# Issuing slot weights and padding from SyncE instead of GpSimd, with fewer VectorE steps in the routing of a two-layer mixture-of-experts block

## The chip, the cores and the metric

One core of a Trainium2 chip runs the whole kernel in one launch. The metric is the device time of that launch in microseconds (us), the median over runs.

## The reference

The input `x` has two sequences of 2048 tokens with 256 channels, all in float32. Three blocks follow one another; the first and the last use the same weights. Layer norms, softmax and gathers are left out here where they only repeat.

```
x = x + 0.5 * ffn(layernorm(x))
x = x + attention(layernorm(x))          # one head, 128 wide, causal
x = x + 0.5 * ffn(layernorm(x))

def ffn(x):                              # 4096 tokens, C = 256
    xln = ln(x, ln1)
    rwkv_state = xln @ Ws
    x = x + (sigmoid(xln @ Wr) * (xln @ Wv)) @ Wo
    h = ln(x, ln2)
    conf = sigmoid(h @ [conf_rwkv, conf_trans])            # 3 confidences
    bids = conf * capital_shares * sigmoid(h @ w_diff) + h @ W_aff
    win = argmax(bids)                                     # one of 3 experts
    wc = conf[win]; scale = wc / (wc + 1e-6)
    out0, out1 = relu(h @ K[e]) ** 2 @ V[e]                # hidden 1024
    out2 = (h @ W1 * sigmoid(rwkv_state @ W2)) @ W3
    return x + out[win] * scale
```

## The kernel before

**Precision.** Each float32 product is made of three passes over fp32r halves (`hi` and `lo`). A value is copied to its `hi` half by ScalarE, and VectorE or GpSimd subtracts to get the `lo` half. `passes` (L428) issues the three matmuls.

**Stages.** One pass of the feed-forward block has a front part, `ffn_a_*`, and a back part, `ffn_b_*`; attention stands between the two passes. The front part goes over eight groups of 512 tokens (`NG` = 8, four tiles of 128 each). It normalizes, makes the gated product, computes the bids and routes: VectorE's `gates(g)` finds the winner, counts it with a scan and casts flags and counts to bf16; TensorE's `prefix(g)` multiplies these with a triangle and with ones, so that each token gets a position; VectorE's `win(g)` computes the gate of the winner and `rank(g)` the row index. GpSimd's `scatter(g)` (L1602) then writes the token rows by four indirect DMAs to `routed`, a DRAM tensor with one region for each expert.

**Back part.** It goes over 18 slots (`NSLOT`), 16 of 256 rows of one expert and two of 128. The first eight (`EARLY_SLOTS`) are planned once five groups (`KNOWN`) are counted, so slots begin while groups 5, 6 and 7 are still routed: the code writes out by hand, on each engine, which step of which group stands between which steps of which slot. For each slot:

- SyncE loads the transposed operand's rows by `z_in(j)` (L1725, tile `slot_z`, semaphore `s_in`) and the residual rows by `row_in(j)` (L1742, tile `slot_row`, semaphore `r_in`). `z_in(0)` waits for the scatters of the first five groups.
- GpSimd loads half of the expert's first weight by `k_in(j)` (L1624, tiles `kx_hi` and `kx_lo`, 512 KB each, two buffers, semaphore `k_in`). It waits until TensorE is through with both halves of slot j-2.
- TensorE runs `sT(j)` (transposes, L770), `K(j, 0)` with weights held in SBUF, `K(j, 1)` with the loaded half, and later `V(j)`, the second product. Its order in the steady part is K(j), sT(j+1), V(j-1).
- ScalarE applies the relu, squares to `hr_hi`, and makes the transposed operand's `hi` half. VectorE computes `relu_squared` (L1463) and the third quarter's gate (L1473, L1475, L1477), the `lo` half of the transposed operand (`slo`, L1454) and the output row (`orow`, L1485 and L1487).
- GpSimd computes `hr_lo` in four quarters (`hrlo(j, n)`, L1674) and sends the output rows by indirect DMA (`send`, L1677). `V(j)` waits for the fourth quarter.

GpSimd's order in slot j from the third on is this; the drain stands there whether a load follows or not.

```
        hrlo(j, 0)
        hrlo(j, 1)
        hrlo(j, 2)
        pool.drain()
        if j + 2 < NSLOT:
            tail.k_in(j + 2)
        hrlo(j, 3)
        send(j - 1)
```

In slots 2 to 5 two tiles of a scatter follow the send, and in slot 5 the padding, `pads()` (L1611): three indirect DMAs of rows from SBUF that mark the end of each expert's region. The pad rows had been loaded to SBUF by SyncE (L1756), in the place of attention weights that come later. The slots from the ninth on need the late table (`late_tiles` to `late_numbers` on VectorE, semaphore `flag`), all scatters and the padding; SyncE waits for these before `z_in(8)`.

VectorE's `win(6)` follows `slo(3)`, and its `rank(6)` follows the gate of slot 2. TensorE's `T2(7)` (L507) waits for that rank. On VectorE a step wrapped in `link` (L1136) is followed by a wait for its own end.

Of the kernel before, what the change touches and what calls it, by code (L numbers as in the profile page):

```python
# [65 lines left out]
def build_kernel(nc, x, w256, w_st, w1, k_w, v_w, w_qkv, ln, shares, ident, tri, mask, tok, table, pad, out):  # L66
    with ExitStack() as ctx:
# [128 lines left out]
        b.oh = sb("winner_one_hot", [P, EXPERTS, GT + 1])  # L196
        b.cs = sb("winner_counts", [P, EXPERTS, GT + 1])
        b.won = sb("winner_conf", [P, EXPERTS, GT])
        b.rk = sb("winner_rank", [P, EXPERTS, GT])
        b.e16 = sb("winner_bf16", [P, EXPERTS * (2 * GT + 1)], BF16)  # L200
# [40 lines left out]
                 "posr", "rowz", "res", "link", "plink", "early", "padi", "pad_in", "flag",  # L241
# [243 lines left out]
def routing_tensor(pe, b, f, s):  # L485
# [645 lines left out]
def routing_vector(dve, b, f, n):  # L1131
# [28 lines left out]
    def gates(g):  # L1160
# [12 lines left out]
        link(dve.tensor_tensor(w(2), w(0), won(2), ALU.max))  # L1173
        link(dve.tensor_scalar(won(0), w(2), 0.5, None, ALU.is_lt))
# [4 lines left out]
        m = EXPERTS * GT  # L1179
        dve.tensor_copy(by_expert(b.e16[:, 0:m]), b.oh[:, :, 1:GT + 1])  # L1180
        dve.tensor_copy(by_expert(b.e16[:, m:2 * m]), b.cs[:, :, 0:GT])
        dve.tensor_copy(b.e16[:, 2 * m:2 * m + EXPERTS], b.cs[:, :, GT]).then_inc(f["e"], 1)

    def win(g):
# [4 lines left out]
        link(dve.tensor_tensor(w(3), b.won[:, 0], b.won[:, 1], ALU.add))  # L1189
        link(dve.tensor_tensor(w(3), w(3), b.won[:, 2], ALU.add))  # L1190
# [363 lines left out]
def ffn_a_gpsimd(pool, b, f, routed, s=None, a=None):  # L1554
# [56 lines left out]
    def pads():  # L1611
        pool.wait_ge(f["padi"], 1)
        pool.wait_ge(f["pad_in"], 16)
        for e in range(EXPERTS):
            pool.indirect_dma_start(routed, bass.IndirectOffsetOnAxis(b.padi[:, e:e + 1].bitcast(U32), 0), b.pad[:], None
                                    ).then_inc(f["padded"], 16)

# [46 lines left out]
def ffn_b_gpsimd(pool, b, f, dst, tail, s=None):  # L1664
# [35 lines left out]
    for j in range(2, NSLOT):  # L1700
# [12 lines left out]
        if j == 5:  # L1713
            tail.pads()
# [748 lines left out]
```

## Time and profile before

| what | value |
|---|---|
| median of 3 runs | 1028.52 us (1027.5 to 1028.8) |
| profiled execution | 1029.34 us |
| its span | 1027.6 us |
| mean granted TensorE clock | 0.95 |
| TensorE matmul busy | 88% of the span |
| VectorE busy | 71% |
| ScalarE busy | 57% |
| GpSimd busy | 54% |

Everything that is counted below comes from the one profiled execution. About 1.7 us of its time lie outside its span. The first feed-forward pass lies at 0 to 409 us, attention at 409 to 640, and the second pass from there to the end; in each pass the front part takes about the first 130 to 155 us.

### The profile page before, as it was taken

How to read it: one execution, taken by the hardware profiler on the slowest of the kernel's cores; microseconds unless marked ns; L12 is line 12 of the kernel's file. 1: busy time of each engine (PE TensorE's matmuls, PEld its weight loads, DVE VectorE, ACT ScalarE, POOL GpSimd, SP SyncE). 2: the span in 40 equal slices, each digit the busy share in tenths (PEclk: the TensorE clock that was granted, in tenths of full speed). 3: DMA queues.
4: the chain of work that ended last, by engine and by line, in shares of the span. 5: the costliest groups of instructions: out<-in, count | busy, mean ns of one | idle time of the engine just before them, and what ended most of it. 6: DMA issues, size and time to landing. Idle time of an engine off the chain costs nothing.

```text
span 1027.6 us, 20302 instructions
## 1 busy us (share of the span) xinstructions
PE 902.7 (88%) x6490; PEld 835.0 (81%) x6490; DVE 733.9 (71%) x1871; ACT 590.2 (57%) x1279; POOL 559.1 (54%) x656
## 2 busy tenths in 40 slices
PE   7998767979899999789998899888868988899997
PEld 6786657978899999678887688667658878899997
DVE  4679988669866664466676677679997769766663
ACT  3776736644566654355653655777756554555663
POOL 3447657866777775551122001256765775777774
PEclk8988988999999999899999999999998999999999
DMA  7215147454565542310111122303236463755542
GB/s 264 114 64 193 63 179 226 145 173 167 202 212 179 166 145 73 94 57 11 63 63 42 42 66 69 113 22 123 119 140 210 145 212 129 240 167 166 165 152 67
DMA packets 72975, 134.58 MB, mean 131 GB/s; under 512 B 7422, under 2 KB 54398, under 8 KB 72704
## 3 DMA queue, kind: packets, MB, share of 16 engines
q0 software_dynamic: 19232, 73.75, 21.1%
q1 hardware_dynamic: 53632, 59.42, 17.8%
q8 instruction: 62, 1.02, 0.4%
q14 instruction: 49, 0.40, 0.1%
HBM read 89.81 MB, written 44.64 MB: 131 GB/s over the span
## 4 chain that ended last, share of the span: by engine, by line
PE 26%; DVE 18%; ACT 5%; issue 4%; POOL 4%; DMA 2%; POOLq 0%; DVEq 0%; SPq 0%; another core or an unknown queue 0%; ACTq 0%
PE bank L431 16%; PE banks4to L431 4%; PE banks4to L2003 3%; DVE pT_lo L2293 2%; ACT p L2163 1%; PE bank L2015 1%; DVE chunk_max L2283 1%; POOL attn_x L2391 1%; DVE relu_squared L1463 1%; DVE state_gate L1475 1%; POOL routed_rows L1608 1%; DVE bn_parts L1362 1%; PE banks4to L770 1%; DMA routed_rows<-out_rows,row_index 1%; ACT pT_hi L2172 1%
## 5 line engine op out<-in xcount | busy, mean ns | idle before, releaser
L1674 POOL TENSOR_TENSOR hr_lo<-relu_squared,hr_hi 128x512 fp32r<-128x512 f32 (+1 forms) x144 | 179.6, 1260 | 65.1 <-DVE relu_squared L1463 53.0
L431 PE MATMUL bank<-v_hi,hr_hi 128*128 x544 | 156.3, 287 | 8.7 <-POOL hr_lo L1674 8.0
L431 PE MATMUL bank<-v_lo,hr_hi 128*128 x544 | 153.4, 282 | 2.8 <-issue 1.7
L431 PE MATMUL bank<-v_hi,hr_lo 128*128 x544 | 153.6, 282 | 0.8 <-issue 0.7
L1463 DVE TENSOR_TENSOR relu_squared<-relu 128x512 f32<-128x512 f32 (+1 forms) x108 | 102.3, 962 | 36.9 <-ACT relu L1023 20.4
L431 PEld LDWEIGHTS bank<-v_hi,hr_hi 128*128 128x128 f32 x544 | 103.5, 190 | 11.0 <-issue 10.9
L1049 ACT CAST hr_hi<-relu_squared 128x512 fp32r<-128x512 f32 (+1 forms) x36 | 21.4, 596 | 148.1 <-DVE relu_squared L1477 148.1
L1454 DVE TENSOR_TENSOR slot_zT_lo<-banks4to,slot_zT_hi 128x512 fp32r<-128x512 f32 (+1 forms) x68 | 42.0, 655 | 89.1 <-ACT slot_zT_hi L1003 79.1
L431 PEld LDWEIGHTS bank<-v_lo,hr_hi 128*128 128x128 f32 x544 | 103.2, 190 | 1.9 <-issue 1.9
L431 PEld LDWEIGHTS bank<-v_hi,hr_lo 128*128 128x128 f32 x544 | 103.5, 190 | 0.8 <-issue 0.6
L1608 POOL DMA_INDIRECT routed_rows<-out_rows,row_index x64 | 66.8, 1043 | 44.7 <-DVE row_index L1205 28.5
L1023 ACT ACTIVATE relu<-bank,slot_k_bias,slot_relu 128x256 f32<-128x256 f32 (+1 forms) x144 | 71.6, 548 | 28.9 <-PE bank L431 13.8
L1570 POOL TENSOR_SCALAR rsqrt_work<-mean_var 128x4 f32<-128x4 f32 x16 | 5.5, 343 | 148.6 <-DVE mean_var L1120 148.4
L431 PE MATMUL bank<-slot_zT_hi,kx_hi 128*128 128x256 f32 (+1 forms) x288 | 82.3, 286 | 0.0
L431 PE MATMUL bank<-slot_zT_hi,kx_lo 128*128 128x256 f32 (+1 forms) x288 | 81.8, 284 | 0.0
L431 PE MATMUL bank<-slot_zT_lo,kx_hi 128*128 128x256 f32 (+1 forms) x288 | 81.4, 283 | 0.0
L2163 ACT ACTIVATE p<-banks4to,minus_row_max 128x512 f32<-128x512 f32 (+2 forms) x80 | 49.8, 629 | 35.4 <-DVE minus_row_max L2286 28.7
L1036 ACT ACTIVATE hr_hi<-relu 128x512 fp32r<-128x512 f32 (+1 forms) x108 | 66.1, 612 | 5.6 <-POOL out_rows L1598 3.4
L2172 ACT CAST pT_hi<-bank 128x512 fp32r<-128x512 f32 (+1 forms) x72 | 39.2, 565 | 39.7 <-PE bank L2015 39.2
L431 PE MATMUL bank<-zT_hi,w_hi 128*128 128x512 f32 x96 | 44.5, 464 | 18.3 <-DVE r_gate L1342 13.1
L2293 DVE TENSOR_TENSOR pT_lo<-bank,pT_hi 128x512 fp32r<-128x512 f32 (+1 forms) x72 | 47.0, 658 | 18.9 <-ACT pT_hi L2172 18.3
L1475 DVE SCALAR_TENSOR_TENSOR state_gate<-relu,slot_relu,state_gate 128x512 f32<-128x512 f32 (+1 forms) x36 | 54.8, 1523 | 1.8 <-ACT relu L1025 0.5
(334 smaller groups left out, 3152.1 us busy)
## 6 DMA issues: line engine op xcount, KB each, us to landing
kx_hi<-first_product_halves POOLq DMA_DIRECT2D x36, 512.0 KB
kx_lo<-first_product_halves POOLq DMA_DIRECT2D x36, 512.0 KB
slot_z<-routed_rows SPq DMA_DIRECT2D x60, 256.0 KB
slot_row<-routed_rows SPq DMA_DIRECT2D x30, 258.0 KB
attn_x<-x_after_ffn SPq DMA_DIRECT2D x16, 256.0 KB, 2.9
attn_out<-x_after_ffn SPq DMA_DIRECT2D x16, 256.0 KB, 2.7
x_after_attention<-attn_out SPq DMA_DIRECT2D x16, 256.0 KB, 2.1
x_rows<-x_after_attention SPq DMA_DIRECT2D x8, 512.0 KB, 4.4
```

What stands on the lines that cost most here:

```text
L431: mm = pe.matmul(outv, w(pw), m(pm), start=(n_first and k == 0), stop=(n_last and k == 2))
L1023: last = act.activation(b.r[n % 2][:, h, 0:m], raw, ACT.Relu, bias=b.kb[:, j, at:at + 1], scale=b.fl[:, j:j + 1])
L1036: act.activation(b.hr[j % 2][0][:, 2 * q:2 * q + 2, 0:m], b.r[n % 2][:, :, 0:m], ACT.Square).then_inc(f["hrhi"], 1)
L1454: dve.tensor_tensor(b.sh[j % 2][1][:, part, :, 0:n], slot_bank(b, j, part).rearrange("p (c n) -> p c n", c=CC)[:, :, 0:n], b.sh[j % 2][0][ ...
L1463: dve.tensor_tensor(b.sq[n % 2][:, :, 0:width(j)], one, one, ALU.mult).then_inc(f["sq"], 1)
L1475: r.link(dve.scalar_tensor_tensor(gate, one, b.fl[:, j:j + 1], gate, ALU.mult, ALU.max))
L1608: pool.indirect_dma_start(routed, bass.IndirectOffsetOnAxis(b.posi[g % 2][:, t:t + 1].bitcast(U32), 0), b.rows[g % 2][:, t, :], None).then ...
L1674: pool.tensor_tensor(b.hr[j % 2][1][:, 2 * q:2 * q + 2, 0:m], b.sq[n % 2][:, :, 0:m], b.hr[j % 2][0][:, 2 * q:2 * q + 2, 0:m].bitcast(F32) ...
L2003: mm = pe.matmul(out[:, at:at + n], b.kq[pw][:, q, 0, t * P:(t + 1) * P], part, start=(k == 0 and i == 0 and not last), stop=(k == 2), ski ...
L2163: act.activation(b.p[s % 2][t][:, c * KEYS:c * KEYS + w], bank(("S", s, t, c))[:, 0:w], ACT.Exp, bias=b.nbias[:, s % 2, t:t + 1], accum_ou ...
L2172: act.copy(b.pT[m % 2][0][:, 0:w], b.bank(m % 2)[:, 0:w]).then_inc(a["pthi"], 1)
L2293: dve.tensor_tensor(b.pT[m % 2][1][:, 0:w], b.bank(m % 2)[:, 0:w], b.pT[m % 2][0][:, 0:w].bitcast(F32), ALU.subtract).then_inc(a["ptlo"], 1)
```

## The change

SyncE takes over `k_in` and `pads` from GpSimd. `k_in(j)` stands behind `z_in(j)` in SyncE's order. `pads` becomes three direct DMAs from DRAM to DRAM, at a row read into a register. The pad rows' copy in SBUF, its load and its semaphore go. In `gates`, the flag of expert 0 is formed in one step from the other two; flags and counts now lie in one tile, which is cast to bf16 by one copy in place of three. `prefix` reads that tile by other views. In `win`, one reduction takes the place of two additions.

```
-    pool.wait_ge(f["early"], 1)
...
-    k_in(0)
     rowz(NG - 2)
-    k_in(1)
     rs2(NG - 2)
...
     hrlo(0, 1)
-    tail.k_in(2)
     hrlo(0, 2)
...
     pool.drain()
-    tail.k_in(3)
     send(0)
     for j in range(2, NSLOT):
         hrlo(j, 0)
         hrlo(j, 1)
         hrlo(j, 2)
         pool.drain()
-        if j + 2 < NSLOT:
-            tail.k_in(j + 2)
         hrlo(j, 3)
         send(j - 1)
...
-        if j == 5:
-            tail.pads()
```

```
+    def k_in(j):
+        e = number(3, j, EXPERTS - 1)
+        if j >= 2:
+            sp.wait_ge(f["Ks"], 4 * (j - 1))
+        for p in range(2):
+            sp.dma_start(b.kx[j % 2][p][:].rearrange("p c n -> p (c n)").bitcast(F32), b.firsts[bass.ds(e * P, P), p].bitcast(F32)
+                         ).then_inc(f["k_in"][j % 2], 16)
+
+    def pads():
+        sp.wait_ge(f["padi"], 1)
+        for e in range(EXPERTS):
+            at = sp.value_load(b.padi[0:1, e:e + 1], min_val=0, max_val=ROWS - P)
+            sp.dma_start(routed[bass.ds(at, P)], pad).then_inc(f["padded"], 16)
+
...
-    sp.dma_start(b.pad[:], pad).then_inc(f["pad_in"], 16)
     sp.wait_ge(f["early"], 1)
     for j in range(2):
         z_in(j)
+        k_in(j)
     for j in range(2):
         row_in(j)
     for j in range(NSLOT - 2):
         if j + 2 == EARLY_SLOTS:
+            pads()
             sp.wait_ge(f["flag"], 1)
             settled(NG)
             sp.wait_ge(f["padded"], 16 * EXPERTS)
             sp.wait_ge(f["pad"], 16)
         z_in(j + 2)
+        k_in(j + 2)
         if j:
             row_in(j + 1)
```

```
-        link(dve.tensor_tensor(w(2), w(0), won(2), ALU.max))
-        link(dve.tensor_scalar(won(0), w(2), 0.5, None, ALU.is_lt))
+        link(dve.scalar_tensor_tensor(won(0), won(2), 0.5, w(0), ALU.is_lt, ALU.is_gt))
...
-        m = EXPERTS * GT
-        dve.tensor_copy(by_expert(b.e16[:, 0:m]), b.oh[:, :, 1:GT + 1])
-        dve.tensor_copy(by_expert(b.e16[:, m:2 * m]), b.cs[:, :, 0:GT])
-        dve.tensor_copy(b.e16[:, 2 * m:2 * m + EXPERTS], b.cs[:, :, GT]).then_inc(f["e"], 1)
+        dve.tensor_copy(b.e16[:], b.ohcs[:]).then_inc(f["e"], 1)
...
-        link(dve.tensor_tensor(w(3), b.won[:, 0], b.won[:, 1], ALU.add))
-        link(dve.tensor_tensor(w(3), w(3), b.won[:, 2], ALU.add))
+        link(dve.tensor_reduce(w(3), b.won[:].rearrange("p e t -> p t e"), AX.X, ALU.add))
```

## Rows read from the trace of the kernel before

**Rows 1.** Busy time by stretch: us, busy time (x instructions) of PE, PEld, DVE, ACT, POOL, then clock, DMA share, GB/s.
```profile
80.00:120.00 40.00, 33.91 (x180) 27.70 (x181) 37.56 (x124) 29.49 (x60) 29.11 (x41) 0.87 0.36 140
...
700.00:720.00 20.00, 17.45 (x99) 14.19 (x98) 19.08 (x67) 13.70 (x27) 15.32 (x21) 0.91 0.46 170
...
920.00:940.00 20.00, 20.00 (x171) 20.00 (x170) 13.44 (x20) 11.35 (x25) 13.84 (x14) 1.00 0.52 168
```
**Rows 2.** What TensorE's matmuls waited for, 760 to 900 us: us in total, times, longest.
```profile
PE bank L431 <- DVE slot_zT_lo L1454: 4.0, 3, 2.4
PE banks4to L507 <- DVE row_index L1205: 3.0, 1, 3.0
PE bank L431 <- POOL hr_lo L1674: 2.9, 2, 2.1
...
PE banks4to L770 <- DMA slot_z<-routed_rows: 2.2, 1, 2.2
```
**Rows 3.** The same in the first pass, 150 to 300 us.
```profile
PE banks4to L507 <- DVE row_index L1205: 4.5, 1, 4.5
...
PE banks4to L770 <- DMA slot_z<-routed_rows: 2.7, 1, 2.7
```
**Rows 4.** The chain that ended last, 690 to 765 us: start us, us, what.
```profile
727.76 0.22 DVE winner_one_hot L1174
...
728.47 0.07 DVE winner_bf L1181
...
729.00 0.17 DVE gate_work L1190
```
**Rows 5.** VectorE's small reduction: count, ns min/median/max, first and last start, form.
```profile
L1246 DVE TENSOR_REDUCE early_slots<-slot_expert_over x2: 154/154/154, 148.9 to 762.7; 128x1 f32<-128x8 f32 x2
```
**Rows 6.** The chain that ended last, from the second pass's first slot load.
```profile
768.25 6.77 DMA slot_z<-routed_rows
```
**Rows 7.** GpSimd in order of time: start us, us, instruction, [idle before].
```profile
767.47 0.60 POOL L1631 DMA_DIRECT2D kx_hi<-first_product_halves  x1 [2.33 <-issue]
```
**Rows 8.** Busy time by stretch at the second pass's first slots, columns as in rows 1.
```profile
768.00:770.00 2.00, 0.07 (x1) 0.07 (x1) 1.98 (x4) 1.96 (x5) 1.96 (x3) 0.50 0.48 81
770.00:772.00 2.00, 2.00 (x9) 2.00 (x10) 2.00 (x5) 0.95 (x2) 2.00 (x3) 0.50 1.02 313
772.00:774.00 2.00, 0.86 (x5) 0.57 (x3) 0.71 (x6) 0.00 (x0) 1.98 (x4) 0.50 1.11 388
```
**Rows 9.** GpSimd in order of time, slots 1 and 2 of the second pass.
```profile
808.13 2.54 POOL L1674 TENSOR_TENSOR hr_lo<-relu_squared,hr_hi 128x512 fp32r<-128x512 f32 x2 [0.83 <-ACT hr_hi L1036]
813.19 0.63 POOL L1631 DMA_DIRECT2D kx_hi<-first_product_halves  x1 [2.52 <-issue]
...
814.70 1.05 POOL L1681 DMA_INDIRECT out_x<-slot_out,token_index  x1 [0.30 <-issue]
...
817.08 2.54 POOL L1674 TENSOR_TENSOR hr_lo<-relu_squared,hr_hi 128x512 fp32r<-128x512 f32 x2
```
**Rows 10.** GpSimd's drain before slot 1's send: ns min/median/max, first and last start.
```profile
L1697 POOLq DRAIN  x2: 3303/3306/3309, 194.5 to 808.6; - x2
```
**Rows 11.** VectorE in order of time, 816 to 868 us: start us, us, instruction.
```profile
817.39 2.26 DVE L1187 CAST out_rows<-tok_sb 128x4 int32<-128x4 f32 x1
...
863.41 3.17 DVE L1284 SCALAR_TENSOR_TENSOR table_work_e<-table_work_e 128x3 f32<-128x3 f32 x1
```
**Rows 12.** The chain that ended last, 880 to 893 us.
```profile
881.25 0.98 POOL routed_rows L1615
...
888.00 1.42 POOLq L1704
...
892.73 1.30 POOL hr_lo L1674
```
**Rows 13.** SyncE's DMA issues in order of time, 886 to 892 us.
```profile
888.87 0.94 SPq L1740 DMA_DIRECT2D slot_z<-routed_rows  x2
```
**Rows 14.** DMA issues by kind, of the page: count, KB each, us from issue to landing.
```profile
routed_rows<-in_pad SPq DMA_DIRECT2D x2, 385.0 KB, 5.6
```

More of the change, by code:

```diff
@@ L195, in build_kernel @@
         b.gw = sb("gate_work", [P, 6, GT])
-        b.oh = sb("winner_one_hot", [P, EXPERTS, GT + 1])
-        b.cs = sb("winner_counts", [P, EXPERTS, GT + 1])
+        b.ohcs = sb("winner_one_hot_counts", [P, 2, EXPERTS, GT + 1])
+        b.oh, b.cs = b.ohcs[:, 0], b.ohcs[:, 1]
         b.won = sb("winner_conf", [P, EXPERTS, GT])
         b.rk = sb("winner_rank", [P, EXPERTS, GT])
-        b.e16 = sb("winner_bf16", [P, EXPERTS * (2 * GT + 1)], BF16)
+        b.e16 = sb("winner_bf16", [P, 2, EXPERTS, GT + 1], BF16)
         b.posi = [sb(f"row_index{i}", [P, GT], I32) for i in range(2)]
@@ L240, in build_kernel @@
                  "x2", "st2", "rs2", "z2", "T2", "hhi", "hlo", "bid", "bd", "bidT", "b7", "conf", "e", "pref",
-                 "posr", "rowz", "res", "link", "plink", "early", "padi", "pad_in", "flag",
+                 "posr", "rowz", "res", "link", "plink", "early", "padi", "flag",
                  "sT", "shi", "slo", "Ks", "relu", "sig", "hrhi", "sq", "hrlo", "Vs", "orow")
@@ L529, in prefix @@
         pe.wait_ge(f["e"], g + 1)
-        pe.matmul(b.bank(5)[:, 0:n], b.tri[:, 0], b.e16[:, 0:n], start=True, stop=False)
-        pe.matmul(b.bank(5)[:, 0:n], b.tri[:, 1], b.e16[:, n:2 * n], start=False, stop=True)
-        pe.matmul(b.bank(5)[:, n:n + EXPERTS], b.tri[:, 1], b.e16[:, 2 * n:2 * n + EXPERTS], start=True, stop=True
+        ahead = b.bank(5)[:, 0:n].rearrange("p (e t) -> p e t", e=EXPERTS)
+        pe.matmul(ahead, b.tri[:, 0], b.e16[:, 0, :, 1:GT + 1], start=True, stop=False)
+        pe.matmul(ahead, b.tri[:, 1], b.e16[:, 1, :, 0:GT], start=False, stop=True)
+        pe.matmul(b.bank(5)[:, n:n + EXPERTS], b.tri[:, 1], b.e16[:, 1, :, GT], start=True, stop=True
                   ).then_inc(f["pref"], 1)
@@ L1609, in scatter @@
                                     b.rows[g % 2][:, t, :], None).then_inc(f["scat"][g % 2], 16)
[L1611 to L1616, printed above, removed]
     def v_lo(first, end):
@@ L1622, in v_lo @@
             pool.tensor_tensor(lo, raw, hi.bitcast(F32), ALU.subtract).then_inc(s.v_lo, 1)
-    def k_in(j):
-        if j == EARLY_SLOTS:
-            pool.wait_ge(f["flag"], 1)
-        e = pool.value_load(b.slots[0:1, 3, j:j + 1], min_val=0, max_val=EXPERTS - 1)
-        if j >= 2:
-            pool.wait_ge(f["Ks"], 4 * (j - 1))
-        for p in range(2):
-            pool.dma_start(b.kx[j % 2][p][:].rearrange("p c n -> p (c n)"), b.firsts[bass.ds(e * P, P), p]
-                           ).then_inc(f["k_in"][j % 2], 16)
     rs1(0)
@@ L1648, in ffn_a_gpsimd @@
             scatter(k - 2)
-    pool.wait_ge(f["early"], 1)
-    if s:
-        for one in s.stored:
-            pool.wait_ge(one, 32)
-    k_in(0)
     rowz(NG - 2)
-    k_in(1)
     rs2(NG - 2)
@@ L1659, in ffn_a_gpsimd @@
     tail = Named()
-    tail.rs2, tail.rowz, tail.scatter, tail.pads, tail.k_in = rs2, rowz, scatter, pads, k_in
+    tail.rs2, tail.rowz, tail.scatter = rs2, rowz, scatter
     return tail
@@ L1687, in ffn_b_gpsimd @@
     hrlo(0, 1)
-    tail.k_in(2)
     hrlo(0, 2)
@@ L1697, in ffn_b_gpsimd @@
     pool.drain()
-    tail.k_in(3)
     send(0)
@@ L1704, in ffn_b_gpsimd @@
         pool.drain()
-        if j + 2 < NSLOT:
-            tail.k_in(j + 2)
         hrlo(j, 3)
@@ L1712, in ffn_b_gpsimd @@
             tail.scatter(last, range(2 * j - 8, 2 * j - 6))
-        if j == 5:
-            tail.pads()
     send(NSLOT - 1)
@@ L1735, in z_in @@
                 if s:
-                    sp.wait_ge(s.stored[EXPERTS - 1], 32)
+                    for stored in s.stored:
+                        sp.wait_ge(stored, 32)
             for part, first in enumerate((0, column)):
```

2 lines of the change are left out of this document (removed).

## The prediction

> **What bounds the kernel now.** I read the busy time by stretch first, because the mean over the span mixes stages with different limits. There the reader sees three kinds of stretch. In the later slots TensorE is busy for all of 20 us at the full clock [rows 1]; the first eight or so slots of each pass do not reach this. In the front parts VectorE is the fullest engine, with 19.08 of 20 us in the second pass and 37.56 of 40 in the first [rows 1]. The start of the slots lies between: TensorE has holes, and the waits name who ends them. In the second pass it waits 2.2 us for the first `slot_z`, 3.0 for `row_index`, 4.0 for `slot_zT_lo` and 2.9 for `hr_lo` [rows 2]; in the first, 2.7 us for `slot_z` and 4.5 for `row_index` [rows 3]. So a saving shows in the front parts if it is VectorE's, at the start of the slots if it shortens one of these waits, and in the dense slots not at all, whatever it takes off GpSimd. Attention has none of the edited steps.
>
> **Routing on VectorE in the front parts.** All steps of `gates` and `win` stand on the chain, back to back. One linked step of the flag goes, 0.22 us [rows 4]. Two of three casts go; in the chain L1181 holds 0.07 us beyond the cast before it, and L1182 as much, together 0.14 [rows 4]. The one cast left has 30 elements and not 12, which I take as free. Two additions become one reduction: one linked step of 0.17 us goes [rows 4], and the reduction is as short as the addition it replaces, by the 0.15 us of a reduction over 8 elements in one output [rows 5]. That is 0.53, rounded to 0.55 us for each group. Five groups are routed in each front part; one of them is followed by a wait for a scatter's landing, where the other engines take the chain. I count four: 4 x 0.55 = 2.2 us for each pass, 4.4 in all. Bounds: two groups (2.2 in all) and, with the three groups inside the slots all on the path, eight (8.8). `prefix` reads the new tile by a strided view in the same number of columns: nothing.
>
> **The first slot's load.** `z_in(0)` brings 512 KB by SyncE's queue, and its second half lands 6.77 us after its issue, at 775.02 us [rows 6]. GpSimd starts its 1 MB of `k_in(0)` at 767.47 us [rows 7], just before, through its own queue. From 768 to 774 us the DMA engines move 2 x (81 + 313 + 388) = 1564 KB [rows 8], which is nearly the sum of both. So the small load that TensorE waits for shares the engines with a large one that it needs later. In the changed order `k_in(0)` is issued behind both parts of `z_in(0)`. Then 512 KB need about 1.5 us at 313 to 388 KB per us after the same start, and land near 772. TensorE finished its earlier work at 775.06 - 2.2 = 772.8. The hole goes: 2.2 us in the second pass, 2.7 in the first [rows 2, 3], 4.9 in all. Bounds: nothing, and 4.9. What is late next are `slo(0)` and then VectorE's work on group 7, both of which follow from the transposes and move with them. `k_in(0)` itself has 1.5 MB to get through and lands near 774, before the second half of K(0).
>
> The Trainium skill, DMA: Bandwidth & Descriptors, section Issuing engines are not separate DMA queues, says that DMAs issued by different engines run on the same 16 engines and interleave, so that another issuer saves only the issue time. By this the first load would land as late as now, and this term would be zero.
>
> **GpSimd freed in slots 1 to 7.** After the last `hr_lo` of slot 1 (808.13 + 2.54 = 810.67) the drain holds until 808.6 + 3.3 = 811.9 [rows 9, 10]. Then come the register load and both halves of `k_in(3)`, until the send is issued, 0.30 us before 814.70: 2.5 us [rows 9]. So the send and the next two `hr_lo` come 2.5 us sooner. These two now start at 817.08 [rows 9], and VectorE's tiny cast in `win(6)`, 0.16 us of work, stands from 817.39 to 819.65, the end of the pair [rows 9, 11]: the two engines exclude each other here. With the pair done by 817.2 the 2.1 us of standing go, and 0.2 us by the reduction. `rank(6)` comes 2.3 us sooner, and TensorE's wait for `row_index` shrinks by that: 2.3 of 3.0 and 2.3 of 4.5 us [rows 2, 3]. Sum 4.6.
>
> In slots 2 to 7 the load stands between the third and the fourth `hr_lo`. In slot 6 the drain ends at 889.42 with the `hr_lo` before it, and the fourth starts at 892.73: 3.3 us [rows 12]. In most slots the fourth quarter's inputs are only ready about when the loads end, so I take 0.9 us a slot as real lead. It shortens VectorE's standing in slots 3 to 5, whose worst piece is 3.17 us in the late table [rows 11], and through it the `slot_zT_lo` waits, 4.0 us [rows 2]. I take 1.8 us a pass, with bounds of 0 and 4. The `hr_lo` waits (2.9) hold 0.9 us at the load of slot 6; without padding, which begins at 881.25 and takes three issues of about 1.3 us before the next `hr_lo`, and without the load, that goes [rows 2, 12]. The 2.1 us in front of it are slot 1's scatter and row work, and stay. I take 0.9 us a pass. Sum of this part: 4.6 + 3.6 + 1.8 = 10.0 us, bounds 2 and 17. In the dense slots GpSimd gets 3 us a slot that TensorE covers: nothing.
>
> **What SyncE takes on.** A pair of loads costs its queue 0.94 us [rows 13] and a register load about as much, 2 us of a slot of 12. In its order `k_in(j+2)` waits for K(j), and the next in line, `row_in(j+1)`, for an output row that is later still; `z_in(j+3)` behind that is needed more than a slot later. Padding: the late table and the last scatter hold `z_in(8)` until 888.87 [rows 13]. The three copies can be issued when SyncE reaches them, near 875; a copy of the pad tile took 5.6 us [rows 14], so they land near 884, hidden. The dropped load into SBUF was hidden too. If this cover failed, `z_in(8)` would be late by some 5 us once a pass, but it has a slot's length before its use.
>
> **Sum.** 4.4 + 4.9 + 10.0 = 19.3 us. The profiled execution has 1029.3 us, 0.8 above the median of the runs: 1029.3 - 19.3 = 1010.0.
>
> **Rivals.** First, *interleaving*: the first `slot_z` is no sooner, since the queue does not keep the order or SyncE's own issue is slow. For it speaks that the loads run on the same DMA engines; against it, that both loads' bytes are counted before the small one lands. 1029.3 - 14.4 = 1014.9. This is what the skill's rule above gives. Second, *VectorE takes over*: what GpSimd frees is lost to VectorE in slots 2 to 7, and only 2 of the 10 us show: 1029.3 - 11.3 = 1018. For it speaks VectorE's late table, which must be done anyway. Third, *more than the holes*: at 768 to 774 us the granted clock is 0.50, the 1.2 GHz level, right after TensorE sat idle [rows 8]. If closed holes keep the clock up, each 2 us of matmuls at the lower level give back 1 us, and the slots' other holes close as well. With 3.5 to 4 us a pass this gives 1002. Fourth, *collisions*, the other side: earlier `hr_lo` pairs meet other small VectorE steps, each a standing of up to 2.5 us [rows 9]. It decides once more than 19.3 / 2.5 = 8 new ones lie on the path of both passes; with ten, 1029.3 - 19.3 + 25 = 1035. Three such places a pass are there already and would have to stay, so this is unlikely. Fifth, *nothing*: SyncE's waits eat the lead and routing was covered: 1028.5.
>
> The Trainium skill, GPSIMD Engine Reference, section Key points, says that GpSimd shares its SBUF interfaces with VectorE and contends with instructions in a two-port mode or with two SBUF inputs. It stands behind the fourth rival; the trace agrees with the sharing, by 2.26 us for a cast of four elements [rows 11].
>
> **How the numbers follow.** Forecast 0.40, interleaving 0.17, VectorE 0.14, more 0.23, collisions 0.03, nothing 0.03. The likeliest case gives 1010 us. From 1000 to 1021 us the range takes in the first three cases, most of the fourth, and leaves out some 0.15. A difference of 0.2%, 2 us, is what a measurement can tell here. Faster by more: 0.94; within: 0.03; slower: 0.03.
>
> **What would show it.** Right: the wait of L770 for `slot_z` is gone in both passes, and that DMA takes some 4 us and not 6.77; `win(6)` has no cast of 2 us; the wait for `row_index` is under 1 us in the second pass and near 2 in the first; in the front parts a group's routing is half a microsecond shorter; the distance from the third `hr_lo` to the fourth falls in the dense slots while their length stays. Wrong: a new wait for `kx_hi` or `kx_lo`, for `slot_row`, or a `z_in(8)` issued later than now; or as many long VectorE steps as before.

## The result, and the profile after

| | before | changed |
|---|---|---|
| median of 5 runs | 1028.8 us (1027.5 to 1032.04) | 1022.02 us (1020.54 to 1024.41) |
| ratio | | 0.994, 95% interval 0.992 to 0.996 |
| profiled execution, its span | 1029.34, 1027.6 us | 1024.41, 1022.6 us |
| mean granted TensorE clock | 0.95 | 0.94 |
| VectorE, GpSimd busy | 733.9, 559.1 us | 706.5, 507.0 us |

The change gained 6.8 us, not the 19.3 forecast, and its 1022 us lie above the end of the forecast's range, 1021. A second comparison, on the chip of the last four experiments, gave 0.9944 (0.993 to 0.9958). VectorE and GpSimd are busy for 27 and 52 us less, so the work did go. One run of e4 below, with 1426 us at a granted clock of 0.55, was in a slower state and is left out of its ratio. What it left behind is read in the same views as before.

Busy time by stretch of the changed kernel, columns as in [rows 1]:
```profile
80.00:120.00 40.00, 34.50 (x182) 27.89 (x182) 36.87 (x118) 29.37 (x58) 30.42 (x45) 0.87 0.40 152
700.00:720.00 20.00, 16.41 (x93) 13.51 (x94) 19.02 (x63) 14.20 (x28) 16.06 (x24) 0.91 0.48 183
920.00:940.00 20.00, 20.00 (x171) 20.00 (x171) 9.92 (x18) 14.10 (x30) 13.53 (x11) 1.00 0.55 161
```
VectorE is still the fullest engine in the front parts, and the dense slots are still 20 of 20 us of TensorE. VectorE has 9.9 us there where it had 13.4 [rows 1]; the two stretches stand differently in the slots' period, so the size says little, but what VectorE is relieved of here TensorE covers.

What TensorE waited for, 760 to 900 us, as in [rows 2]:
```profile
PE bank L429 <- DVE slot_zT_lo L1448: 7.4, 3, 4.3
PE banks4to L429 <- DVE gT_lo L1342: 5.0, 1, 5.0
PE bank L429 <- POOL hr_lo L1645: 4.6, 1, 4.6
```
And 150 to 300 us, as in [rows 3]:
```profile
PE bank L429 <- DVE slot_zT_lo L1448: 9.6, 3, 4.5
PE banks4to L429 <- DVE gT_lo L1342: 4.8, 1, 4.8
PE bank L429 <- POOL hr_lo L1645: 3.7, 1, 3.7
```
The waits for `slot_z` and for `row_index` that the prediction aimed at are gone from both lists: 2.2 + 3.0 us in the second pass and 2.7 + 4.5 in the first [rows 2, 3]. In their place stand one longer wait for `hr_lo` and longer ones for `slot_zT_lo`: 12.0 us of these two in the second pass against 4.0 + 2.9 before [rows 2]. The wait for `gT_lo` stands ahead of the first slot and was there before with 4.7 and 4.6 us. All waits in these two stretches sum to 21.2 us where they were 23.9 in the first pass, and to 20.7 where they were 21.7 in the second. So most of the idle time was moved, not removed. Three places make it up.

**Slot 1, the landing of a scatter.** SyncE's and GpSimd's instructions in order of time:
```profile
790.92 0.35 SPq L1723 DMA_DIRECT2D kx_hi<-first_product_halves  x1
791.46 0.34 SPq L1723 DMA_DIRECT2D kx_lo<-first_product_halves  x1
```
```profile
790.64 1.36 POOL L1602 DMA_INDIRECT routed_rows<-out_rows,row_index  x1 [0.16 <-issue]
...
794.84 0.96 POOL L1602 DMA_INDIRECT routed_rows<-out_rows,row_index  x1 [0.31 <-issue]
795.83 2.53 POOL L1645 TENSOR_TENSOR hr_lo<-relu_squared,hr_hi 128x512 fp32r<-128x512 f32 x2
802.46 3.25 POOL L1592 TENSOR_SCALAR out_rows<-x_rows,rsqrt_work 128x256 f32<-128x256 f32 x4 [4.10 <-DMA routed_rows<-out_rows,row_index]
806.54 2.49 POOL L1645 TENSOR_TENSOR hr_lo<-relu_squared,hr_hi 128x512 fp32r<-128x512 f32 x2 [0.83 <-ACT hr_hi L1035]
```
`k_in(3)` is now issued at 790.9, beside the four scatters of group 5; before, GpSimd itself issued it at 813.19 [rows 9], long behind them. `rowz(7)` (L1592), in which GpSimd scales the rows of group 7, needs the scatter's source tile and waits 4.10 us; the scatter lands 802.46 - 795.80 = 6.7 us after the end of its last issue. Before, that row work started 0.29 us behind the pair of `hr_lo`:
```profile
802.88 4.41 POOL L1598 TENSOR_SCALAR out_rows<-x_rows,rsqrt_work 128x256 f32<-128x256 f32 x4 [0.29 <-DMA routed_rows<-out_rows,row_index]
```
Behind it on GpSimd is the pair of `hr_lo` for which V(1) waits: 4.60 us at 805.2 and 3.66 in the first pass, where it was 2.06 in both.

**Slot 7, the late numbers.** VectorE and GpSimd, 875 us:
```profile
875.14 2.88 DVE L1205 TENSOR_SCALAR slot_relu<-slot_expert_over 128x11 f32<-128x11 f32 x1
```
```profile
875.46 2.51 POOL L1645 TENSOR_TENSOR hr_lo<-relu_squared,hr_hi 128x512 fp32r<-128x512 f32 x2
```
The first step of `late_numbers`, 11 elements, stands until the pair of `hr_lo` ends; the same step took 0.27 us before, when the three issues of padding, from 881.25 on, held that pair back to 884.81 and the numbers were done at 883.2:
```profile
880.64 0.27 DVE L1211 TENSOR_SCALAR slot_relu<-slot_expert_over 128x11 f32<-128x11 f32 x1
```
Behind it in VectorE's order stands `slo(7)`, and TensorE waits 4.32 us (4.48 in the first pass) for it.

**Slot 1 in the first pass, VectorE's `lo` half.** The first transposes start at 156.53 and not at 161.56, but TensorE then waits 3.2 us at 169.9 for `slo(1)`, which VectorE makes behind the statistics of group 7, `win(5)` and a square. Busy time by stretch, the changed kernel, then the kernel before:
```profile
160.00:168.00 8.00, 6.73 (x60) 6.62 (x58) 7.35 (x27) 7.00 (x15) 4.07 (x5) 1.00 0.91 287
168.00:174.00 6.00, 4.08 (x19) 4.09 (x20) 5.78 (x13) 3.27 (x8) 3.88 (x5) 0.58 0.67 230
174.00:180.00 6.00, 6.00 (x43) 5.87 (x43) 3.70 (x5) 3.81 (x8) 2.00 (x2) 0.86 0.01 3
```
```profile
160.00:168.00 8.00, 6.44 (x42) 6.44 (x43) 4.53 (x19) 4.20 (x9) 5.37 (x7) 0.79 1.00 322
168.00:174.00 6.00, 4.38 (x40) 4.28 (x40) 5.79 (x21) 4.44 (x10) 3.77 (x6) 1.00 0.13 27
174.00:180.00 6.00, 6.00 (x51) 6.00 (x52) 5.80 (x12) 5.16 (x12) 3.75 (x5) 1.00 0.85 255
```
The reader is to see two things. VectorE is full (5.78 of 6 us at 168 to 174). And the granted clock is 0.58 and 0.86 behind the wait, at 168 to 180 us, where it was 1.00 before; the kernel before had its stretch at the 1.2 GHz level earlier, behind the wait for `slot_z` (0.79 at 160 to 168). From the transposes of slot 0 to those of slot 9, the sum of (1 - clock) x time is 6.8 us before and 13.0 after in the first pass (9.7 and 8.8 in the second), while the idle gaps of TensorE behind the first transposes, so without the hole for `slot_z`, sum to 15.8 before and 16.4 after (14.0 and 15.0). In the first pass the lead of 5.0 us at the first transposes is gone at V(1), which starts at 197.55 us and before started at 197.40.

The transposes came 5.0 us sooner, but the lead of VectorE's work behind them shrank on the way. VectorE and GpSimd of the changed kernel, then VectorE before:
```profile
160.39 0.74 DVE L1164 TENSOR_TENSOR expert_bids<-conf_rows,shares_sb 128x12 f32<-128x12 f32 x1 [0.28 <-ACT conf_rows L878]
161.16 1.22 DVE L1165 TENSOR_TENSOR expert_bids<-expert_bids,conf_rows 128x12 f32<-128x12 f32 x1
```
```profile
158.56 3.79 POOL L1609 TENSOR_TENSOR v_lo<-raw_v_lo,v_hi 128x512 fp32r<-128x512 f32 x3
```
```profile
164.77 0.86 DVE L1165 TENSOR_TENSOR expert_bids<-conf_rows,shares_sb 128x12 f32<-128x12 f32 x1 [0.28 <-ACT conf_rows L879]
165.66 0.17 DVE L1166 TENSOR_TENSOR expert_bids<-expert_bids,conf_rows 128x12 f32<-128x12 f32 x1
```
The second of these steps of 12 elements now stands until GpSimd's three `v_lo` end at 162.35, 1.05 us longer than before. This too is a new standing; no run took it off by itself.

### The profile page after: what moved, and what is told of

It reads as the page before. It is cut to its first block, busy times and chain, and to the rows that moved or that the text cites. A ratio compares the mean times of both kernels' runs of the same rounds, so it can differ in the third digit from the quotient of the medians.

```text
span 1022.6 us, 20262 instructions
## 1 busy us (share of the span) xinstructions
PE 905.9 (89%) x6490; PEld 837.9 (82%) x6490; DVE 706.5 (69%) x1807; ACT 591.0 (58%) x1279; POOL 507.0 (50%) x578
## 4 chain that ended last, share of the span: by engine, by line
PE 32%; DVE 14%; ACT 6%; issue 4%; POOL 3%; DMA 1%; DVEq 0%; another core or an unknown queue 0%; ACTq 0%; POOLq 0%; SPq 0%
PE bank L429 18%; PE banks4to L429 6%; PE banks4to L1985 4%; PE bank L1997 2%; DVE pT_lo L2275 2%; ACT p L2145 1%; DVE chunk_max L2265 1%; POOL attn_x L2373 1%; ACT relu L1022 1%; DVE state_gate L1469 1%; PE banks4to L769 1%; ACT pT_hi L2154 1%; DMA routed_rows<-out_rows,row_index 1%; DVE relu_squared L1457 1%; DVE bn_parts L1356 1%
## 5 line engine op out<-in xcount | busy, mean ns | idle before, releaser
L1457 DVE TENSOR_TENSOR relu_squared<-relu 128x512 f32<-128x512 f32 (+1 forms) x108 | 80.5, 751 | 53.9 <-ACT relu L1022 32.9
L429 PE MATMUL bank<-slot_zT_hi,k_hi 128*128 128x256 f32 (+1 forms) x144 | 44.3, 308 | 17.2 <-DVE slot_zT_lo L1448 16.9
```

The source lines that it names most:

```text
L429: mm = pe.matmul(outv, w(pw), m(pm), start=(n_first and k == 0), stop=(n_last and k == 2))
L1457: dve.tensor_tensor(b.sq[n % 2][:, :, 0:width(j)], one, one, ALU.mult).then_inc(f["sq"], 1)
```

## The experiments

All were timed in 5 rounds, each against the kernel before on the same chip. Beside the ratio stands a length from the trace, that of the slots: from the start of the last step of `rank(4)` to the start of the last slot's transposes, in each pass, 244.6 and 245.1 us before.

| kernel | ratio, 95% interval | first pass | second |
|---|---|---|---|
| changed | 0.994, 0.992 to 0.996 | 245.5 | 241.2 |
| the same again (e14) | 0.9944, 0.993 to 0.9958 | 244.6 | 241.8 |
| e1 routing alone | 0.9952, 0.9924 to 0.998 | 244.3 | 243.9 |
| e2 SyncE's part alone | 0.9976, 0.9957 to 0.9996 | 245.8 | 241.3 |
| e3 hold | 0.9884, 0.9858 to 0.9909 | 242.6 | 239.0 |
| the same again (e16) | 0.9887, 0.9868 to 0.9905 | 240.8 | 239.1 |
| e4 padding on GpSimd | 0.9903, 0.9864 to 0.9941 | 242.3 | 239.0 |
| e5 both | 0.984, 0.9826 to 0.9853 | 238.8 | 237.5 |
| the same again (e13) | 0.9869, 0.9853 to 0.9886 | 239.9 | 237.5 |
| e6 hold and order at slot 6 | 0.9885, 0.987 to 0.9901 | 238.6 | 237.7 |
| e7 hold, first loads mixed | 0.9914, 0.9897 to 0.993 | 241.0 | 242.0 |
| e8 hold and order at slot 1 | 0.9928, 0.9914 to 0.9943 | 241.5 | 241.1 |
| e9 both and order at slot 6 | 0.9914, 0.9888 to 0.994 | 243.0 | 240.1 |
| the same again (e15) | 0.9936, 0.9918 to 0.9954 | 243.1 | 240.6 |
| e10 both and idle matmuls | 0.988, 0.9854 to 0.9907 | 242.2 | 237.9 |
| e11 hold, load also at its old place | 0.9926, 0.9897 to 0.9954 | 242.1 | 239.9 |
| e12 both, without the routing edits | 0.9904, 0.987 to 0.9939 | 243.2 | 237.2 |

**e1 and e2: the two parts of the change.** e1 is the kernel before with the third diff block of the change alone, e2 the changed kernel without it.

> The kernel before with the routing edits alone (one linked flag step, one cast for three, one reduction for two additions). Theory A, the routing steps lie on the path in both front parts as summed (4.4 us): ratio 0.9957, near 1024.4 us, and the distance of two row_index steps in the front parts shorter by 0.5 us each. Theory B, the front part's end is held by other waits, so that a saving of 0.5 us a group is lost by the last group: the ratio is 0.998 to 1.0, and the second pass's row_index of the fifth group comes no more than 1 us sooner relative to the first.

> The changed kernel without its routing edits: weights and padding by SyncE alone. If the forecast's 14.9 us for this part held, the ratio would be 0.9855. Theory: most of that is given back at two places inside the slots (the fourth hr_lo of slot 1 behind a slow scatter, and the late table behind a pair of hr_lo), so the ratio is 0.995 to 0.997, and TensorE shows both waits, about 4.5 us each, in the second pass.

Routing alone gives 0.9952, some 4.9 us; SyncE's part alone 0.9976, 2.5 us with an interval of 0.4 to 4.4, where the prediction had 14.9. In e2's trace the `slot_z` and `row_index` waits are gone and the new ones are there: 3.6 and 4.56 us for `hr_lo`, 4.70 and 4.27 for `slot_zT_lo` at slot 7.

**e3, e11: the load beside the scatter.** `settled(n)` waits until the scatters of the first n groups have landed. e3:
```
         if j >= 2:
             sp.wait_ge(f["Ks"], 4 * (j - 1))
+        if j == 3:
+            settled(NG - 2)
         for p in range(2):
```

> The changed kernel, where SyncE holds the third slot's weight load until the scatter of group 5 has landed. Theory, collision on the DMA engines: that load of 1 MB, issued at 790.9 us beside the scatter of 790.6 to 795.8, is what makes the scatter land 6.6 us after its last issue in place of 2.9. Then here it lands in under 3.5 us, TensorE's wait for hr_lo in slot 1 falls from 4.6 to about 2 us in the second pass and from 3.7 to 2 in the first, and the time falls by 3 to 4 us against the changed kernel: ratio 0.990 to 0.991. Rival, the scatter is slow for another reason (all the slots' loads together): the wait stays at 4.6 and the ratio at 0.994.

In the trace of e3, GpSimd in order of time:
```profile
788.61 0.96 POOL L1602 DMA_INDIRECT routed_rows<-out_rows,row_index  x1 [0.30 <-issue]
789.59 2.54 POOL L1645 TENSOR_TENSOR hr_lo<-relu_squared,hr_hi 128x512 fp32r<-128x512 f32 x2
792.14 4.70 POOL L1592 TENSOR_SCALAR out_rows<-x_rows,rsqrt_work 128x256 f32<-128x256 f32 x4
```
`rowz(7)` starts right behind the pair: the scatter has landed 2.6 us after its last issue or sooner. V(1)'s wait is 2.1 us again (1.9 in the first pass). Here 2.2 us of the wait for `row_index` come back in the second pass and 0.8 in the first (0.8 and 2.0 in e16), and it still gains 5.8 us over the changed kernel by the difference of the ratios, in both comparisons, more than the 3 to 4 expected. e11 keeps the hold and loads the same 1 MB once more where the changed kernel has it:
```
         if j == 3:
+            for p in range(2):
+                sp.dma_start(b.kx[j % 2][p][:]...).then_inc(f["twice"], 16)
+            sp.wait_ge(f["twice"], 32)
             settled(NG - 2)
```

> The kernel with the hold, and in addition the third slot's weights are also loaded once at the place where the changed kernel loads them, ahead of the hold (the same 1 MB into the same tiles, then again behind the hold). Theory A (it is the bytes of this load beside the four scatters of group 5 that make them land late): GpSimd's rows of group 7 wait again some 4 us for the scatter's landing, TensorE's wait for hr_lo at slot 1 is 4 to 4.6 us in the second pass and not 2.1, ratio back to 0.992 to 0.996. Rival B (what follows the load in SyncE's order, the slot rows and the next slot_z, is what the hold kept away): no wait of GpSimd for the landing, hr_lo wait near 2.1 us, ratio 0.987 to 0.990.

GpSimd in e11:
```profile
788.17 0.96 POOL L1602 DMA_INDIRECT routed_rows<-out_rows,row_index  x1 [0.30 <-issue]
789.14 2.55 POOL L1645 TENSOR_TENSOR hr_lo<-relu_squared,hr_hi 128x512 fp32r<-128x512 f32 x2
795.41 3.21 POOL L1592 TENSOR_SCALAR out_rows<-x_rows,rsqrt_work 128x256 f32<-128x256 f32 x4 [3.72 <-DMA routed_rows<-out_rows,row_index]
```
Landing 6.3 us after the last issue, V(1) waiting 3.68 and 4.13 us, ratio 0.9926: theory A. It is the load's bytes beside the scatter's, not what follows in SyncE's order.

**e4, e5: the padding.** e4 is the changed kernel with the pad tile and its load as before, and this; e5 is e3 and e4 together.
```
         if j in (2, 3):
             tail.scatter(last - 1, range(2 * j - 4, 2 * j - 2))
         elif j in (4, 5):
             tail.scatter(last, range(2 * j - 8, 2 * j - 6))
+        if j == 5:
+            tail.pads()
...
         if j + 2 == EARLY_SLOTS:
-            pads()
             sp.wait_ge(f["flag"], 1)
```

> The changed kernel with the padding issued by GpSimd again, after slot 5's scatter. Theory, exclusion on VectorE: three issues of 1.3 us hold the pair of hr_lo of slot 6 back until the late table's last part is through, so its first step is 0.3 us and not 2.9, and TensorE's wait for slot_zT_lo there falls from 4.3 to 2 us; the pair then ends later, and that may cost up to 1 us at the next product. Net 0 to 2 us faster a pass: ratio 0.991 to 0.994. Rival, padding by SyncE was the gain that was forecast (0.9 us a pass): ratio 0.995 to 0.997.

> The changed kernel with both repairs: SyncE holds the third slot's weight load until the scatter of group 5 has landed, and the padding is issued by GpSimd again. Additive theory (two separate holes, one at slot 1 by the landing of the scatter, one at slot 7 by the pair of hr_lo standing in front of VectorE's late numbers): 0.9884 for the hold alone and 0.0037 less for the padding, a ratio near 0.985; the wait for slot_zT_lo at slot 7 falls from 4.5 to about 2.6 us in both passes, that for hr_lo at slot 1 stays near 2. Rival (the two act on the same wait, or the hole only moves on): no better than the hold alone, 0.987 to 0.990.

VectorE and GpSimd in e4:
```profile
869.20 0.26 DVE L1207 TENSOR_SCALAR slot_relu<-slot_expert_over 128x11 f32<-128x11 f32 x1
```
```profile
869.79 0.99 POOL L1611 DMA_INDIRECT routed_rows<-pad_rows,pad_row_index  x1 [0.30 <-issue]
871.08 0.96 POOL L1611 DMA_INDIRECT routed_rows<-pad_rows,pad_row_index  x1 [0.30 <-issue]
872.35 0.97 POOL L1611 DMA_INDIRECT routed_rows<-pad_rows,pad_row_index  x1 [0.30 <-issue]
873.34 2.52 POOL L1654 TENSOR_TENSOR hr_lo<-relu_squared,hr_hi 128x512 fp32r<-128x512 f32 x2
```
The pair starts 3.9 us behind the last issue of the scatter and not at once, the first late number takes 0.26 us, and the wait at slot 7 is 2.8 and 2.6 us. The hr_lo wait at slot 1 stays (3.6 and 4.4). Both together reach 0.984, just as the additive theory had it. To see whether that was a lucky draw, e13 (the same kernel as e5), e14 (the changed kernel), e16 (the hold) and e15 (as e9) ran beside each other.

> Hold and padding on GpSimd, the same kernel as e5, beside the changed kernel on the same chip. If the two new waits account for the missing term: 0.984 to 0.986, 8 to 10 us under the changed kernel. If the earlier 0.984 was a fast draw: 0.987 to 0.991, 3 to 7 us under it.

> The changed kernel itself, as a base for the other three. From its first comparison: 0.992 to 0.996; hr_lo wait at slot 1 of 4 to 4.6 us and slot_zT_lo wait at slot 7 near 4.4 us in the second pass, as in its first profile.

> The hold alone, the same kernel as e3: 0.987 to 0.990, 4 to 6 us under the changed kernel, if the landing of the scatter is worth what its first comparison gave; under 2 us below it if that was the draw.

Both repairs: 0.9869, 1015.2 us beside 1023.7 for the changed kernel. By the difference, 8.4 us, this is the first case; the ratio itself falls between the two ranges. The slots' lengths repeat within 1.8 us in the first pass of the hold and within 1.1 us elsewhere. So the repairs bring 8 to 10 us: about 6 by the hold, 2 to 4 by the padding. The padding's part is a difference of two ratios, each uncertain by some 2 us, so its size is less sure than the hold's; its mechanism is read from the trace.

**e7: the first load alone.** With the hold, the first slot's two weight halves are issued between the two halves of its rows:
```
                 sp.dma_start(b.sz[p][:, part, t:t + m], rows...)
+                if j == 0:
+                    sp.dma_start(b.kx[0][part][:]..., b.firsts[...]).then_inc(f["k_in"][0], 16)
```

> The changed kernel with the hold, and the two halves of the first slot's weights issued between the two halves of its rows, as they fell before. Prediction's term (the hole of 2.2 and 2.7 us in front of the first transposes is worth its length, 4.9 us): the ratio rises from 0.9884 to 0.993. Theory now (the time won there is lost again at slot 1, where TensorE waits 3.15 us for VectorE's lo half in the first pass, and at half clock): the first transposes come about 2 us later in both passes, the wait at slot 1 is 1 to 2 us shorter in the first pass, ratio 0.988 to 0.990.

The waits at the start of the first pass's slots in e7:
```profile
PE banks4to L769 <- DMA slot_z<-routed_rows: 1.6, 1, 1.6
PE bank L429 <- DVE slot_zT_lo L1448: 1.4, 1, 1.4
```
The hole for `slot_z` is back with 1.6 us (1.5 in the second pass), and the one for `slo(1)` is 1.4 and not 3.16. So e7 brings back 3.1 us of a hole that was 4.9 in both passes. In time it costs 0.9914 against 0.9884 and 0.9887: 3 us, with some 3 us of uncertainty on this difference. It decides between neither of the two theories. The lengths in the table say more: the first pass is as long as with the hold alone (241.0 against 242.6 and 240.8), since what was won at the first load is waited for at `slo(1)`; in the second the order of the issues is worth 3 us (242.0 against 239.0 and 239.1).

**e6, e8, e9: VectorE's order.** e8 makes `slo(1)` ahead of `win(5)` and of the second square; e6 makes `slo(7)` ahead of `late_numbers`:
```
     r.stats2(last)
+    slo(1, 0)
+    slo(1, 1)
     r.win(last - 2)
     sq(0, 1)
-    slo(1, 0)
-    slo(1, 1)
```
```
-        elif j == 6:
-            r.late_numbers()
         if j + 1 < NSLOT:
             slo(j + 1, 0)
             slo(j + 1, 1)
+        if j == 6:
+            r.late_numbers()
```

> The changed kernel with the hold, and VectorE makes the lo half of slot 1's operand ahead of the gate of group 5's winner and of the second square, not behind them. Theory A (VectorE's order is what took over the time won at the first load; each microsecond of such a hole brings about as much again at half clock behind it): the wait of 3.15 us in the first pass falls to 1 to 1.5, the stretch of 8 us at half clock behind it (168 to 175 us) shortens, 3 to 5 us in all, ratio 0.984 to 0.986. Rival B (the second square is later, so hr_lo and the rank of group 5 are, and TensorE waits there): 0.987 to 0.991.

> The changed kernel with the hold, and in slot 6 VectorE makes the lo half of slot 7's operand before the late numbers and not behind them. Theory A (the wait for slot_zT_lo of 4.5 and 4.3 us is VectorE's order: the first late number stands 2.9 us behind a pair of hr_lo, and the lo half stands behind that): the waits fall under 1.5 us, the stretches at half clock behind them go as well, 4 to 5 us a pass, ratio 0.979 to 0.981. Rival B (the hole moves: the 5 us of late numbers now stand in front of the third square and the gate of slot 6, and TensorE waits as long for hr_lo or a free bank): 0.986 to 0.990.

In e8 the wait at slot 1 does fall to 1.9 us in the first pass, but the one for `hr_lo` grows to 2.7 (1.9 and 2.1 in e3 and e16) and that for `row_index` to 2.3 (0.8 and 2.0), and it is 4 us slower than the hold alone: the mechanism of rival B, with a loss beyond its range. In e6 the wait at slot 7 falls from 4.3 and 4.5 to 1.8 and 2.3 us, and its slots are shorter in the one profile, yet the ratio is that of the hold alone: nothing that can be measured, as rival B had it. The profiled execution was the fastest of e6, 1013.5 us beside a median of 1016.4, so its slots may be shorter than usual; why they do not show in the ratio stays open.

> Hold, padding on GpSimd, and in slot 6 the lo half of slot 7's operand ahead of the late numbers. Theory A (with the pair of hr_lo held back by the padding, the late numbers take 2.9 us and not 5.5, so the order alone wins most of the remaining wait of 2.6 and 2.75 us at slot 7): ratio 0.981 to 0.982 against 0.984 without it. Rival B (as in the kernel with the order alone, what is won at slot 7 is lost at the third square and gate behind it): 0.983 to 0.986.

> The same kernel as e9 (both repairs and the order at slot 6). If the order takes time away, since the slot_z of slot 8 is issued behind the flag and TensorE waits 2.3 to 3.4 us for it: 2 to 7 us slower than both repairs alone. If the order is neutral and the earlier 0.9914 was the chip: within 2 us of them.

In both of its comparisons (0.9914, 0.9936) this order takes away most of what the two repairs brought, which neither theory of e9 had. The first pass of e15 shows where, SyncE's issue and the transposes of slot 8:
```profile
268.03 0.95 SPq L1717 DMA_DIRECT2D slot_z<-routed_rows  x2
```
```profile
271.57 1.75 PE L771 MATMUL banks4to<-ident_sb,slot_z 128*128 128x128 f32 x7 [3.66 <-DMA slot_z<-routed_rows]
```
`z_in(8)` needs the flag that `late_numbers` sets and the landing of the padding; TensorE, earlier at slot 7, is now there at 267.9 and waits 3.66 us (2.24 in the second pass). This is the next bound behind the one removed. The profiled executions of e15 and e9, 1015.4 and 1015.5 us, are faster than their medians, 1022.6 and 1021.2, so these waits are a part of the loss and what slows the others is not seen.

**e10: the clock.** e5 with idle matmuls in the wait for `gT_lo` ahead of slot 0:
```
     r.bidT(last - 2)
+    for _ in range(34):
+        pe.matmul(b.bank(1)[:, 0:CC * P], b.Wb[:, 0], b.Wb[:].rearrange("p c n -> p (c n)"), start=True, stop=True)
     Wo(last, range(0, 2))
```

> Hold, padding on GpSimd, and 34 idle matmuls of 128x256 (0.12 us each at full clock, 4.1 us) in the wait of 4.6 to 4.9 us for gT_lo that stands ahead of the first slot in both passes; they write a bank that nobody reads. Theory A (a hole costs its length and then half the time of a stretch of about 6 us at the 1.2 GHz level): the granted clock stays near 1.00 from 154 to 160 and from 762 to 768 us, 3 us a pass; part of it is taken by the first load, which lands when it does, and by VectorE at slot 1: 2 to 5 us in all, ratio 0.979 to 0.982 against 0.984. Rival B (the clock falls all the same, or all of it is waited for again at slot 1): 0.983 to 0.986.

The stretch behind that wait in e10, then in e5:
```profile
156.00:160.00 4.00, 1.93 (x15) 1.52 (x13) 3.75 (x11) 2.03 (x5) 3.60 (x5) 1.00 0.66 149
```
```profile
156.00:160.00 4.00, 4.00 (x19) 4.00 (x20) 2.76 (x9) 1.37 (x3) 2.46 (x4) 0.50 0.97 305
```
The clock stays at 2.4 GHz, TensorE needs 1.93 us there and not 4.00, and the time is not shorter: 0.988 against 0.984 and 0.9869, longer than either theory had it. TensorE now waits 1.4 us for `slot_z` again and 3.9 us at slot 1 in the first pass, where the profile names `relu`. Up to slot 1 of the first pass the load and the steps of the other engines set the pace, and a faster TensorE waits longer there: rival B. In the second pass the first transposes come 12.5 us behind the last step of `rank(4)` and not 13.9, and the whole pass is no shorter (237.9 against 237.5).

**e12: SyncE's part, repaired, without routing.** e2 with the edits of e3 and e4.

> SyncE's part alone with both repairs: the weights issued by SyncE with the hold, the padding by GpSimd, and VectorE's routing as in the kernel before. Additive theory (routing 0.9952 by itself, all three 0.984): 0.984 / 0.9952 = 0.9888, that is 11.5 us of which the prediction had 4.9 for the first load and 10 for GpSimd's freed time; the waits for hr_lo at slot 1 near 2 us and for slot_zT_lo at slot 7 near 2.6 us. Rival (the repairs only work with the shorter routing, since VectorE is what TensorE waits for at slots 0 and 1): 0.992 to 0.996, with a wait for slot_zT_lo at slot 1 of over 3 us in the first pass and a stretch at half clock behind it.

The ratio is 0.9904 with an interval of 0.987 to 0.9939, which holds the additive 0.9888 and a part of the range of the rival. The waits for `hr_lo` at slot 1 are 2.1 and 2.0 us. The one at slot 7 is 1.2 and 2.8. The rival's mark is there too: 3.7 us for `slo(1)` in the first pass, with the half clock behind it. So it leans to the additive theory and does not exclude a part for VectorE.

## Why the prediction was wrong

**Routing** (4.4 us): right, as far as it can be told. e1 measures 4.9 us with an interval of 2 to 8. From `winner_one_hot` to `row_index` the same group takes 731.42 - 727.29 = 4.13 us before and 728.61 - 725.06 = 3.55 after, 0.58 shorter against 0.55. The chain of the changed kernel has the new steps at the prices taken:
```profile
725.34 0.17 DVE winner_one_hot_counts L1172
...
725.82 0.18 DVE winner_bf L1177
...
726.18 0.18 DVE gate_work L1184
```
The cast of 30 elements is 0.18 us where that of 12 was 0.17, and the reduction is as short as an addition.

**The first slot's load** (4.9 us): the mechanism was right, its size held in one pass only. From `rank(4)` to the first transposes it takes 156.53 - 142.64 = 13.9 us in the first pass and 772.50 - 757.85 = 14.65 in the second, where it took 16.3 and 16.0: 2.4 and 1.4 us of the holes of 2.7 and 2.2. In e2, which has the routing of before, it is 13.7 us in both passes, the full length of the holes. By e7 the order of the issues is worth some 3 us, and by the slots' lengths all of it lies in the second pass. The step that failed is "what is late next are `slo(0)` and then VectorE's work on group 7, both of which follow from the transposes and move with them". In the first pass the transposes moved by 5.0 us and VectorE's work on group 7 by 3.8 (its residual at 163.81 and not 167.59), most of the difference being the standing under `v_lo`, and `slo(1)` stands behind it. TensorE waits 3.2 us there, with the lower clock behind it. The rival *interleaving* is refuted. In e3, whose trace has the landings, the halves of `slot_z` are issued at 760.67 and 761.27 us and those of `k_in(0)` at 762.42 and 762.96; 760 to 764 us, median from issue to landing:
```profile
slot_z<-routed_rows SPq DMA_DIRECT2D x2, 256.0 KB, 2.9
kx_hi<-first_product_halves SPq DMA_DIRECT2D x1, 512.0 KB, 4.5
kx_lo<-first_product_halves SPq DMA_DIRECT2D x1, 512.0 KB, 5.5
```
Two loads on the same DMA engines, but the one issued first landed first.

The Trainium skill, DMA: Bandwidth & Descriptors, section Issuing engines are not separate DMA queues, says that another issuer saves only the issue time. That rule gives no gain for this term. What this case changed beside the issuer is the order and the moment of the issues, and e7 measures some 3 us for the order alone.

**GpSimd freed** (10 us): this term failed, and it is the one that made the sum wrong. e2's 2.5 us less e7's 3 leave nothing for it, within some 4 us. Its first half looks as written: no cast of `win` takes more than 0.77 us, where `win(6)`'s took 2.26, and the wait for `row_index` is gone in both passes, more than the 2.3 us each that were forecast. Part of this is only that TensorE now comes late from V(1): with that wait taken off, e3 waits 0.8 and 2.2 us for `row_index`, e16 2.0 and 0.8. Two steps in it were wrong, both of one kind: the work that was taken away had been holding something back.

- "Then come the register load and both halves of `k_in(3)`" counted what the load costs GpSimd, and "what SyncE takes on" what it costs SyncE's queue. It did not ask what 1 MB issued 22 us earlier would meet. It met the scatter on which `rowz(7)` and with it V(1) depend. e3 takes this off and gains 5.8 us, e11 puts it back.
- "Without padding, and without the load, that goes": the `hr_lo` wait of slot 6 did go, 0.9 us. But the padding was also what kept a pair of `hr_lo` from standing in front of the late numbers. e4 shows the 2.88 us step as 0.26, and the padding's return is worth 2 to 4 us.

With both repaired, e5 and e13 give 16.5 and 13.5 us by their ratios. Less 4.9 for routing and 3 for the first load, 8.6 and 5.6 remain of the 10: a fair size, though each term taken off is uncertain by some 3 us, hidden by two new waits.

**The rivals.** *Collisions* had half of the mechanism and the wrong threshold. It asked for eight new standings; one at slot 7 in each pass and a collision that it did not name, of two transfers at slot 1, were enough, since each lay in front of the step that TensorE needs next. *VectorE takes over* named 1018 us and is right for slot 1 of the first pass, where TensorE waits for `slo(1)`. *More than the holes* counted the clock as a bonus only. It is as much a price: in the profiles of the changed kernel (and of e14) each wait of 3.2 to 4.6 us at slots 1 and 7 has about 7 us at the lower level around it and behind it, where the waits behind the first transposes had about 3.5 us or none before, and the first pass's slots did not get shorter at all (245.5 and 244.6 against 244.6). The sum took each wait off by itself; it has to be made again once the order has moved.

## What to carry to other kernels

When an engine gives up a DMA or an issue, list what that instruction held back, not only what it cost: the transfer now starts when its buffer comes free, and may meet a small one that somebody waits for; the engine's next instruction now starts at once, and may stand in another engine's way. A large load whose use is far off can be tied to the landing of the small transfer that is urgent. And when a wait is removed, name the next one with its length before counting the gain: here the first waits that were removed gave most of their length to the next ones, and making `slo(1)` or `slo(7)` earlier brought no time.

## What the runs showed of the hardware

- A scatter of four indirect DMAs landed 2.9 us after the end of its last issue in the kernel before and within 2.6 in e3, and after 6.3 and 6.7 us with a 1 MB load issued beside it (e11, the changed kernel).
- A step of 11 elements on VectorE took 2.88 us when a pair of two-input GpSimd steps began 0.3 us behind it, and 0.26 us without. It ended at 878.02 us and the pair at 877.97; the cast of four elements of the kernel before ended at 819.65 and its pair at 819.62 [rows 9, 11].
- VectorE's squares (128x512 at most, 108 of them) fell from 962 to 751 ns on average in the changed kernel, with the same median of 691 ns in both, 22 of the 27 us that its busy time lost. So most of what VectorE was relieved of is standing, not work. Which of the edits does this was not taken apart.
- Waits of equal length are not always followed by the lower clock. TensorE waited 3.66 us in e4 (to 169.61 us) and 3.69 us in e5 (to 172.11) in the same place of the first pass, at `slo(1)`. Behind it the clock was in e4, and then in e5:
```profile
172.00:176.00 4.00, 4.00 (x27) 4.00 (x26) 2.73 (x3) 1.71 (x5) 0.91 (x1) 0.69 0.05 15
```
```profile
172.00:176.00 4.00, 3.89 (x33) 3.89 (x34) 3.84 (x8) 1.39 (x4) 2.27 (x2) 1.00 0.48 167
```
  In e5 the level stayed at 1.00 on to 207 us. What decides it was not tried. It may be one reason why the same kernel differs by 2 to 4 us and more from run to run.
